# Router logits and dt as fp32 products by rows in four column groups, turned back by a 0/1 selection product, in a new instruction order

## The reference, cut to what matters

```python
h = _layernorm(x) * (1 + ca) + sa
zxbcdt = h @ W_in                      # z 512, xBC 768, dt 8 columns
xBC = silu(causal_dwconv(xBC, conv_w, conv_b))
dt = softplus(dt + dt_bias)            # per head
y = ssd(x, dt, A, B, C) + x * D        # scan over the sequence
y = rms_norm(y * silu(z)) @ W_out
x = x + ga * y
h = _layernorm(x) * (1 + cb) + sb
gate = softmax(h @ gate_w + gate_b)    # 8 columns
weights = gate * (gate >= 0.1);  weights /= sum(weights)
x = x + gb * sum_e weights[e] * (h @ expert_w[e] + expert_b[e])
```

## Time and profile before

| | |
|---|---|
| median of the runs | 2277.26 us |
| the profiled execution | 2272.85 us, its span 2270.8 us |
| PE busy | 2181.3 us, 96% |
| DVE busy | 1893.8 us, 83% |
| ACT busy | 1788.6 us, 79% |
| POOL busy | 1620.3 us, 71% |
| granted TensorE clock, mean | 0.973 |

### The profile page before, as it was taken

How to read it: one execution, slowest core, us unless ns; L and a number is a source line. 1 busy time by engine, 2 the same in 40 slices (tenths; PEclk the granted TensorE clock), 3 DMA queues, 4 the chain that set the end, 5 groups by cost and what they waited for, 6 DMA issues and landing times. The chain is left out here.

```text
span 2270.8 us, 48650 instructions
## 1 busy us (share of the span) xinstructions
PE 2181.3 (96%) x14808; PEld 1874.0 (83%) x14808; DVE 1893.8 (83%) x4196; ACT 1788.6 (79%) x4208; POOL 1620.3 (71%) x1810
## 2 busy tenths in 40 slices
PE   4679999999999999999999999999999999999997
PEld 3568888888888888888888888888888888888875
DVE  4778898888898888898888889888889888889873
ACT  2678778888878788887788877788877788887872
POOL 1546777777777777777777777777777777777775
PEclk9789999999999999999999999999999999999999
DMA  4222122122122122122222212222212212212210
GB/s 119 70 71 67 60 78 80 59 79 83 58 69 83 60 82 79 58 66 83 70 73 78 71 60 78 70 70 78 79 57 73 83 58 83 80 57 67 73 54 19
DMA packets 154257, 160.86 MB, mean 71 GB/s; under 512 B 17200, under 2 KB 136592, under 8 KB 154000
## 3 DMA queue, kind: packets, MB, share of 16 engines
q1 hardware_dynamic: 148848, 157.71, 22.6%
q10 hardware_dynamic: 5152, 0.04, 0.1%
HBM read 139.88 MB, written 17.83 MB: 69 GB/s over the span
## 5 line engine op out<-in xcount | busy, mean ns | idle before, releaser
L897 DVE SCALAR_TENSOR_TENSOR feat<-pa,cw,feat 128x512 f32<-128x512 f32 x567 | 422.9, 746 | 39.2 <-ACT feat L603 24.8
L1300 PE MATMUL pe<-e_hi,h_hi 128*128 128x512 f32 x1024 | 450.7, 440 | 3.9 <-ACT ex L746 2.1
L1300 PE MATMUL pe<-e_hi,h_lo 128*128 128x512 f32 x1024 | 413.6, 404 | 0.0
L1300 PE MATMUL pe<-e_lo,h_hi 128*128 128x512 f32 x1024 | 412.5, 403 | 0.0
L1300 PE MATMUL pa<-h_hi,w_hi 128*128 128x260 f32 x1260 | 383.5, 304 | 10.3 <-DVE feat L897 9.1
L1300 PE MATMUL pa<-h_lo,w_hi 128*128 128x260 f32 x1260 | 357.5, 284 | 0.0
L1300 PE MATMUL pa<-h_hi,w_lo 128*128 128x260 f32 x1260 | 357.4, 284 | 0.0
L675 ACT ACTIVATE lm<-lm,lndt 128x128 f32<-128x128 f32 x1024 | 327.3, 396 | 1.7
L665 ACT ACTIVATE lm<-lm,e3in 128x128 f32<-128x128 f32 x1024 | 323.2, 403 | 4.1 <-DMA lm<-cs_rows 4.1
L1096 DVE SCALAR_TENSOR_TENSOR eacc<-pe,wg,eacc 128x256 f32<-128x256 f32 x512 | 245.0, 478 | 51.1 <-PE pe L1300 39.5
L439 POOL TENSOR_TENSOR rs<-ssq,neghalf 128x1 f32<-128x1 f32 x128 | 80.8, 632 | 280.3 <-DVE ssq L1004 280.3
(11 more groups left out here) (181 smaller groups left out, 6041.3 us busy)
## 6 DMA issues: line engine op xcount, KB each, us to landing
lm<-cs_rows SPq DMA_DIRECT2D x128, 512.0 KB, 3.9
ebc<-cs_rows SPq DMA_DIRECT2D x256, 128.0 KB, 3.0
xin<-_attn_hidden_states_dram SPq DMA_DIRECT2D x32, 512.0 KB, 4.1
xres<-_attn_hidden_states_dram SPq DMA_DIRECT2D x128, 128.0 KB, 3.3
out_dram<-x SPq DMA_DIRECT2D x128, 128.0 KB, 3.4
gz<-in_L_wmod_dram SPq DMA_DIRECT2D x2, 512.0 KB, 9.1
ex<-in_L_ffn_expert_w_dram SPq DMA_DIRECT2D x1, 1024.0 KB, 16.3
x<-in_L_ffn_expert_w_dram SPq DMA_DIRECT2D x1, 1024.0 KB, 17.8
```

The lines of the kernel that those rows point to most:

```text
L897: dve.scalar_tensor_tensor(out=acc, in0=proj_bank(x, i)[:, :, 1 + j:1 + j + HT], scalar=cw[:, f, j:j + 1], in1=acc, op0=ALU.mult, op1=ALU. ...
L1300: return pe.matmul(o, lhsT=l, rhs=r, start=start, stop=stop, skip_group_check=True)
```

## The change

The narrow projections are turned round. The fp32 weights, 8 columns padded with zeros to 32, are now what stays in the array, and 128 tokens move past them (`by_rows`): for a pair, 2 tiles x 2 halves of the features, each in its own group of 32 columns, so that the four results lie in 32 partitions each of one PSUM tile. ACT copies this tile to SBUF (`dte` into a part of `xin` that has been read, `lge` into a part of `xn2`). One more fp32 matmul with the 0/1 matrix `sel` (`dt2`, `lg2`) turns it back to tokens on partitions and adds the two halves. DVE then adds the bias in one operation. `dtm` now works per pair, as `lgm_` does, so a group has four products by rows, four copies and four selection products. They read `hf` and `h2f`, not the split parts: `dtm` no longer waits for `n_hi` and `n_lo` (`ft0` does), and the next `n_h` and `h2` wait until their source has been read. `hT_` puts all its four transposes into one bank of `pa`, the other bank takes the product and the selection. `nabs` shares the buffer `w1`. The transfer into `xin` waits for `dt2`, no longer for `hT`. The splits of `wdt` and `g_hl` in the start are dropped. The lists of steps are in a new order on all five engines.

```diff
             def load_xin(sp, x):
                 if x.g >= 1:
-                    sp.wait_ge(S["hT"], 2 * x.g)
+                    sp.wait_ge(S["dt2"], 2 * x.g)
...
+            pool.memset(wdt[:, :, NH:32], 0.0).then_inc(POOL0.sem, 1)
+            pool.memset(wgate[:, :, NE:32], 0.0).then_inc(POOL0.sem, 1)
...
                 if x.pair >= 1:
                     act.wait_ge(S["n_hi"], x.pair)
                     act.wait_ge(S["n_lo"], x.pair)
+                    act.wait_ge(S["dtm"], x.pair)
                 for k in range(KT):
-                    last = act.activation(hf[:, k], pa[:, k, 0:HT], ACT.Identity,
+                    last = act.activation(hf[:, k], pa[:, 0, k * HT:(k + 1) * HT], ACT.Identity,
...
+            def dte(act, x):
+                act.wait_ge(S["dtm"], x.pair + 1)
+                act.activation(xin[:, x.t, 0:P], pa[:, 1, 0:P], ACT.Copy).then_inc(S["dte"], 1)
...
+            def lge(act, x):
+                act.wait_ge(S["lgm"], x.pair + 1)
+                act.activation(xn2[:, 0, 0:P], pd[:, 0, 0:P], ACT.Copy).then_inc(S["lge"], 1)
...
             def dtb(dve, x):
-                hl = pa[:, 0, 0:2 * T * NH].rearrange("p (t a h) -> p t a h", t=T, a=2)
-                dve.wait_ge(S["dtm"], x.g + 1)
+                dve.wait_ge(S["dt2"], x.pair + 1)
                 if x.g >= 1:
                     dve.wait_ge(S["dts"], 4 * x.g)
-                dve.tensor_tensor(v[:], hl[:, :, 1], rep(dtb_rep[:], T, NH), ALU.add).then_inc(S["dtb"], 1)
-                dve.wait_ge(S["dtb"], 2 * x.g + 1)
-                dve.tensor_tensor(v[:], hl[:, :, 0], v[:], ALU.add).then_inc(S["dtb"], 1)
+                dve.tensor_tensor(v[:, x.t:x.t + 2], pa[:, 1, P:P + 2 * NH].rearrange("p (t h) -> p t h", t=2), rep(dtb_rep[:], 2, NH),
+                                  ALU.add).then_inc(S["dtb"], 1)
...
-            dve.tensor_copy(g_hl[:, :, 0:NE], gate_f[:]).then_inc(DVE0.sem, 1)
-            dve.wait_ge(DVE0.sem, DVE0.at["ghi"])
-            dve.tensor_tensor(g_hl[:, :, NE:2 * NE], gate_f[:], g_hl[:, :, 0:NE].bitcast(F32), ALU.subtract).then_inc(DVE0.sem, 1)
...
+            def by_rows(o, w, h):
+
+                for a in range(2):
+                    for k in range(KT):
+                        part = slice((2 * a + k) * 32, (2 * a + k + 1) * 32)
+                        last = mm_(o[part, 0:P], w[:, k], h[:, k, a * P:(a + 1) * P], True, True)
+                return last
+
             def dtm(pe, x):
-                pe.wait_ge(S["n_hi"], 2 * (x.g + 1))
-                pe.wait_ge(S["n_lo"], 2 * (x.g + 1))
-                pe.wait_ge(S["n_h"], 2 * (x.g + 1))
-                if x.g == 0:
-                    pe.wait_ge(DVE0.sem, DVE0.at["dlo"])
-                for t in range(T):
-                    tok = slice(HALO + t * P, HALO + (t + 1) * P)
-                    for k in range(KT):
-                        for i, h in enumerate((h_hi, h_lo)):
-                            last = mm_(pa[:, 0, 2 * t * NH:2 * (t + 1) * NH], h[:, x.q, k, tok], wdt[:, k], k == 0 and i == 0, k == KT - 1 and i == 1)
-                last.then_inc(S["dtm"], 1)
+                if x.n == 0:
+                    loaded(pe, s_dt)
+                    pe.wait_ge(POOL0.sem, POOL0.at["zdt"])
+                pe.wait_ge(S["n_h"], x.pair + 1)
+                if x.pair >= 1:
+                    pe.wait_ge(S["dtb"], x.pair)
+                by_rows(pa[:, 1], wdt, hf).then_inc(S["dtm"], 1)
+
+            def dt2(pe, x):
+                if x.n == 0:
+                    pe.wait_ge(DVE0.sem, DVE0.at["sel"])
+                pe.wait_ge(S["dte"], x.pair + 1)
+                mm_(pa[:, 1, P:P + 2 * NH], xin[:, x.t, 0:P], sel[:].rearrange("p a h -> p (a h)"), True, True).then_inc(S["dt2"], 1)
...
                     if i == 0:
                         pe.wait_ge(S["dtb"], 2 * (x.g + 1))
+                        pe.wait_ge(S["n_hi"], 2 * (x.g + 1))
+                        pe.wait_ge(S["n_lo"], 2 * (x.g + 1))
...
-                pe.wait_ge(S["h2hi"], x.pair + 1)
-                pe.wait_ge(S["h2lo"], x.pair + 1)
-                for j in range(2):
-                    for k in range(KT):
-                        for i, h in enumerate((h2_hi, h2_lo)):
-                            last = mm_(pd[:, 0, 2 * j * NE:2 * (j + 1) * NE], h[:, x.pair % NH2, k, j * P:(j + 1) * P], g_hl[:, k],
-                                       k == 0 and i == 0, k == KT - 1 and i == 1)
-                last.then_inc(S["lgm"], 1)
+                    loaded(pe, s_exp)
+                pe.wait_ge(S["h2e"], x.pair + 1)
+                by_rows(pd[:, 0], wgate, h2f).then_inc(S["lgm"], 1)
+
+            def lg2(pe, x):
+                pe.wait_ge(S["lge"], x.pair + 1)
+                mm_(pd[:, 0, P:P + 2 * NE], xn2[:, 0, 0:P], sel[:].rearrange("p a h -> p (a h)"), True, True).then_inc(S["lg2"], 1)
...
+                do(dtm, pe, n + 2, T)
+                do(lgm_, pe, n - 6)
```

More of the change, by code:

```diff
@@ L180, in adaln_mamba_moe @@
         S = {name: sem(name) for name in (
-            "hT", "dtm", "ft", "z", "cs", "G", "xT", "yoff", "ydiag", "state", "wout", "ss", "h2T", "lgm", "wgT", "bias", "expD", "expA", "gt",
-            "n_h", "cacc", "gzs", "silu", "u", "ln", "lndt", "e3", "csTe", "L", "Lx", "bt", "xt", "sq", "y_hi", "h2e", "gexp", "wTe",
+            "hT", "dtm", "dt2", "ft", "z", "cs", "G", "xT", "yoff", "ydiag", "state", "wout", "ss", "h2T", "lgm", "lg2", "wgT", "bias", "expD", "expA", "gt",
+            "n_h", "dte", "cacc", "gzs", "silu", "u", "ln", "lndt", "e3", "csTe", "L", "Lx", "bt", "xt", "sq", "y_hi", "h2e", "lge", "gexp", "wTe",
             "biasE", "exA", "gtE",
@@ L762, in _ @@
             do(n_h, act, 0)
+            do(dte, act, 0)
             do(n_h, act, 2)
+            do(dte, act, 2)
             do(exp_u, act, 0)
@@ L790, in _ @@
             for n in range(0, NTILE + 16, T):
-                do(yhi_, act, n - 8)
-                do(xA1, act, n - 13)
+                do(h2, act, n - 10)
                 do(n_h, act, n - 2, T)
                 do(La, act, n - 6)
+                do(lge, act, n - 10)
+                do(xA1, act, n - 13)
+                do(dte, act, n - 2, T)
+                do(gexp, act, n - 12)
+                do(Lxa, act, n - 6)
+                do(yhi_, act, n - 7)
+                do(gtE, act, n - 12)
@@ L1031, in xn2_ @@
                 if x.n >= 2:
-                    dve.wait_ge(S["h2T"], x.pair)
+                    dve.wait_ge(S["lg2"], x.pair)
                 dve.tensor_scalar(xn2[:, x.j], x2[:, x.n % NX2], mv2[:, x.j, 0:1], rstd2[:, x.j:x.j + 1],
@@ L1133, in _ @@
             do(dtb, dve, 0)
+            do(dtb, dve, 2)
             do(nabs_, dve, 0)
@@ L1446, in h2T_ @@
                 else:
[L1447 removed]
+                    pe.wait_ge(S["lg"], x.pair)
                 for k in range(KT):
@@ L1525, in _ @@
             do(hT_, pe, 0)
+            do(dtm, pe, 0)
             do(hT_, pe, 2)
-            do(dtm, pe, 0)
+            do(dt2, pe, 0)
+            do(dtm, pe, 2)
+            do(dt2, pe, 2)
             do(ft0, pe, 0)
@@ L1545, in _ @@
             mm_(py[:, 0], ident[0:NB, 0:1].to_broadcast([NB, P]), grow, True, True).then_inc(PE0.sem, 1)
-            for n in range(0, NTILE + 12, T):
-                do(ss_, pe, n - 8)
-                do(ydiag_, pe, n - 7)
-                do(xT_, pe, n - 6)
-                do(gt_, pe, n - 12)
-                do(G_, pe, n - 6)
-                do(lgm_, pe, n - 10)
-                do(dtm, pe, n - 4, T)
-                do(e0, pe, n - 12)
+            for n in range(0, NTILE + 16, T):
+                do(state_, pe, n - 7)
+                do(lg2, pe, n - 10)
+                do(dt2, pe, n - 2, T)
+                do(G_, pe, n - 6)
+                do(gt_, pe, n - 12)
+                do(ss_, pe, n - 8)
```

397 lines of the change are left out of this document (196 added, 201 removed).

## The result

The changed kernel takes 2303.47 us (median of 4 runs, 2298.7 to 2307.56), the kernel before beside it 2276.95 (4 runs): ratio 1.0111, 95% interval 1.0093 to 1.013. It is 1.1% slower where 2.2% faster was forecast. The profiled execution took 2298.7 us, its span is 2297.0, the mean granted clock 0.992 after 0.973.

A forecast was written before the change was run, and what follows sets the result against it. The prediction took TensorE (PE) as the bound. Work -21, clock -40, added wait +15 and start -5 sum to -51 us, 2226 us from the median 2277.26; own range 2205 to 2245, 8 in 10 for 2190 to 2266.

The forecast's parts named there:

- The step that failed: In some 30 of 32 groups, TensorE (PE) is the bound; a microsecond taken from it counts nearly in full.
- The wait at the edge: At the group's edge, PE waits at the second `dt2` for ACT: some 0.5 us a group, 15 us added.
- Rival 2: Slower: ACT sets the pace at the group's edge, with 4.1 us of waiting a group; 2334 us, chance 0.06.
- PE's own work: In each group, thin matmuls go, products by rows and selections come: 0.7 us less, 21 us in 30 groups.
- The clock: In the steady stage, 23 or 24 drops to half clock beside 24 thin matmuls go: 40 us less.
- Rival 1: The clock still falls once a group, at the group's edge; 2266 us, chance 0.11.
- Rival 3: Slower: the column groups do not overlap in the products by rows; 2308 us, chance 0.04.
- The start: Before the first groups, a wait for the low half and gate-weight operations go: 5 us less (4 to 8).

The follow-up runs named there:

- half_thin: Kernel before, order untouched, with the low-half products of dt and of the router's logits left out: 2229.38 us, ratio 0.9807.
- split_run: Kernel before with one step moved, the 16 thin dt matmuls behind the expert product that followed them: 2276.81 us, ratio 1.0004.
- old_order: Changed kernel's steps put into the order of the kernel before, with some layer-norm steps of the input later: 2293.21 us, ratio 1.008.
- lg_rows: Kernel before, in its order, with only the router's logits by rows; dt keeps its 16 thin matmuls: 2260.96 us, ratio 0.9932.
- dt_rows: old_order with the logits as in the kernel before and only dt by rows: 2311.65 us, ratio 1.0156.
- dt_apart: dt_rows with the dt products, selections and a ScalarE copy moved away from what they wait for: 2281.61 us, ratio 1.0014.
- three reliefs: Changed kernel with expert terms left out of each group's first tile (2292.9 us) or fourth tile (2283.35), or five convolution taps on VectorE narrowed (2283.27).
- fix5: fix3 with two more moves, sums earlier on VectorE and a decay-row load earlier on SyncE: 2293.88 us, ratio 1.0082.
- fix3: Changed kernel in its own order with four local moves, on TensorE and VectorE, of steps TensorE was seen waiting for: 2305.54 us, ratio 1.0128.
- both_apart: old_order, both products by rows, with the dt steps moved as in dt_apart: 2287.47 us, ratio 1.0051.

## Why the prediction was wrong

**The step that failed** is in the first part: "So for some 30 of the 32 groups of four tiles PE is the bound: a microsecond taken from it counts nearly in full there". PE was the bound, as the chain of the kernel before says (1386 of 1400 us), but only just. half_thin gave back 45 of 105 us, 32 of it the clock's part: a group of 66.1 us without a drop lost 1.8 us of work and got no shorter than about 66.0. So even with no new wait the 21 us of work were hardly to be had, and the 40 of the clock only where nothing else came late. A busy share of 99.6% says who is the bound, not how far below it the next one lies. The other engines' shares (83 to 87%) say nothing of it either: the next bound was no engine but a loop. In the changed kernel it takes 68.2 us a group, 2.1 more than the 66.1 that PE needed, with 16 us of DVE in it that have no idle time.

**The wait at the edge** was forecast at one place, the second `dt2`, at 0.5 us, found by counting ACT's work against PE's from `h2T_` on. In the changed kernel that wait is there, once a group and smaller: 0.21 us at the weight load, 7.6 us in all where the sum had 15. But 2.4 us a group of others came with it (59.8 us idle in 25 groups of 1700 us, 6.8 before), which the sum had at nothing. I followed PE's queue at the edge and not what ACT and DVE get later when PE's order changes. Rival 2 had the price about right ("It decides above 66 / 30 = 2.2 us of waiting a group") and the place and the chance, 0.06, wrong; and its engine too, since ACT holds 153 of the 1400 us of the chain.

**PE's own work** was sized too dear. With its way in, a lone product by rows takes 0.44 us (0.09 and the 0.35 behind 1172.86) where the sum had 0.56, the two that follow each other 0.67 (0.09, 0.25, 0.33) where it had 0.93; the selection takes 0.23 to 0.25 where I took 0.22. Four products come to about 1.55, the selections to 1.0, so some 1.1 us less a group and not 0.7. That is the low end of the bounds (0.45 and 0.71): the eight passes run four abreast, 2 x 0.115 = 0.23, and the fixed cost read off `ydiag_` is there, 0.21 for a lone product and 0.21 once for the two. The rule of the Trainium skill that I set beside it, on the drain in TensorEngine Tiling (Array Packing), section Key Properties, agrees with where the 0.21 lies: 0.09 in front and 0.10 to 0.12 behind, at the change to and from full-width matmuls, and 0.02 between the products at 1177.92 and 1178.17, where the mode stays.

**The clock** went as forecast: one drop between 400 and 2100 us where there were 20, granted clock 1.00. Its 40 us were not paid out. In split_run the clock is up as well and the time is that of the kernel before; in half_thin, where nothing came later than before, it was paid. Rival 1 is out. **Rival 3** is out by the 0.25 us. **The start** was sized at 5 us: the first gate transpose starts 11.3 us earlier (158.5 after 169.8), in old_order 6.6. How much of it is the new order and how much the dropped work and wait is not shown. So the miss lies in the groups: 36.8 us more, where 46 less were forecast. (In the chances, rival 1 is counted with 0.10 and 0.02 where it has 0.11, and the slower side with 0.09 where it has 0.10.)

**What is shown and what is not.** Shown: in the old order the loss is on the dt side (lg_rows against dt_rows), and 30 us of it are the close handovers at the group's edge (dt_apart). What the later layer-norm steps, which dt_rows and dt_apart share, add to it is not shown. Shown too, by three reliefs, that in the changed kernel neither PE nor DVE alone sets the pace (ACT was relieved in old_order only); which round does is read from the trace, and fix5, whose moves were to shorten it, won 12 us on fix3. That the dt handovers are what makes the changed kernel slow in its own order is not shown. Nor is it shown how much of the changed kernel's 2303 us is the new order itself: with the old order the same steps take 2293, so 10 us at least in this pair, but no run has the old products in the new order. Why both_apart keeps 11 us over before while lg_rows and dt_apart keep -15 and 5 is open as well, though the loop that bounds it is known. The best kernel measured is lg_rows, 2260.96 us, 0.7% faster than the kernel before and 1.8% faster than the changed one.

## What to carry to other kernels

In a kernel with a written-out order, the busiest engine's saving is worth only the distance to the next loop: here 0.1 to 0.3 us of the 1.8 taken from a group in half_thin. Before forecasting a gain, leave some of its work out in place and see what comes back; and look in the trace for stretches in which another engine has no idle time, whatever its share. A step that is turned from one instruction into a handover to another engine and back costs little where its result is old, and holds up everything queued behind it where that engine is the late one. When a removed wait turns up elsewhere at the same length, stop chasing waits and look for the loop.
